# Layer block on one core: a new prologue, a new order in the two short steps, and reciprocals spread by one float32r product

## The reference

```
a   = layernorm(x)
q, k, v = a Wq + bq, (a Wk + bk) Wc We, (a Wv + bv) Wc We      # 16 query heads, 4 key/value heads of 16
qf, kf  = elu(q) + 1, elu(k) + 1
num = einsum(qf, cumsum_t(kf * v));  den = einsum(qf, cumsum_t(kf)) + 1e-6
y   = a + (num / den) Wo + bo
x2  = x + layernorm(y) * gamma + beta
z   = layernorm(x2);  zs = z shifted by one token
xr  = mu_r z + (1 - mu_r) zs;  xk likewise with mu_k
out = x2 + sigmoid(xr W_r^T) * (relu(xk W_k^T)^2 W_v^T)
```

## Time and profile before

| | |
|---|---|
| median of 3 runs | 298.79 us (298.68 to 300.03) |
| the profiled execution's own time | 300.61 us |
| its span in the trace | 298.8 us |
| PE, PEld busy | 272.9 us (91%), 192.7 us (65%) |
| DVE busy | 235.1 us (79%) |
| ACT, POOL busy | 145.4 us (49%), 128.8 us (43%) |
| mean granted TensorE clock | 0.969 |
| chain that ended last | PE 76%, DVE 10%, ACT 5%, issue 3%, DMA 2% |

### The profile page before, as it was taken

One profiled execution on the slowest core, in us unless ns is written; L12 is line 12 of the kernel. 1 busy time (PEld: TensorE's weight loads), 2 busy tenths in 40 slices (PEclk: granted clock), 3 DMA queues, 4 the chain that ended last, 5 costly groups with the idle time before them and its releaser, 6 DMA issues.

```text
span 298.8 us, 7425 instructions
## 1 busy us (share of the span) xinstructions
PE 272.9 (91%) x2923; PEld 192.7 (65%) x2923; DVE 235.1 (79%) x578; ACT 145.4 (49%) x294; POOL 128.8 (43%) x151
## 2 busy tenths in 40 slices
PE   7598798887899999999999999999999999977894
PEld 7565655745685578756885588557865677654663
DVE  6629569799799959996899779985999558989433
ACT  1238655545454756376455844484247520453540
POOL 2711660244474447436753567354344414063310
PEclk9789799997799999999999999999999999999999
DMA  6900202002000013000400020001100110002012
GB/s 175 274 12 3 72 1 72 2 3 70 3 2 0 2 37 105 2 3 3 140 2 0 2 73 0 2 2 35 37 5 0 37 37 2 0 0 71 35 37 70
DMA packets 12178, 10.73 MB, mean 36 GB/s; under 512 B 2288, under 2 KB 12144, under 8 KB 12144
## 3 DMA queue, kind: packets, MB, share of 16 engines
q1 hardware_dynamic: 11392, 9.97, 10.5%
q10 hardware_dynamic: 752, 0.30, 0.4%
HBM read 6.07 MB, written 4.19 MB: 34 GB/s over the span
## 4 chain that ended last, share of the span: by engine, by line
PE 76%; DVE 10%; ACT 5%; issue 3%; DMA 2%; ACTq 1%; POOL 1%; DVEq 0%
PE ps_x L448 9%; PE ps_x L478 8%; PE ps_x L370 7%; PE ps_x L463 6%; PE ps_z L419 6%; PE ps_x L470 6%; PE ps_y L440 5%; PE ps_x L364 5%; PE ps_y L435 5%; PE ps_z L470 4%; PE ps_x L456 2%; PE ps_z L463 2%; PE ps_x L357 2%; DVE probs L953 2%; PE ps_z L402 2%
## 5 line engine op out<-in xcount | busy, mean ns | idle before, releaser
L953 DVE TENSOR_TENSOR probs<-ps_z,causal 128x512 f32<-128x512 f32 x64 | 40.8, 679 | 6.7 <-PE ps_z L419 6.7
L273 POOL TENSOR_TENSOR out_tok<-tanh_r,x_tok 128x512 f32<-128x512 f32 x14 | 18.7, 1338 | 27.7 <-DVE tanh_r L1026 27.7
L1026 DVE SCALAR_TENSOR_TENSOR tanh_r<-tanh_r,ps_x 128x512 f32<-128x512 f32 x13 | 8.9, 687 | 27.0 <-PE ps_x L478 27.0
L448 PE MATMUL ps_x<-wo_sb,oT 128*128 128x256 f32 x128 | 29.6, 382 | 0.0
L250 POOL TENSOR_TENSOR xb_tok<-x_in,beta_bc 128x1024 f32<-128x1024 f32 x8 | 18.9, 2361 | 24.8 <-DVE x_tok L999 24.8
L370 PE MATMUL ps_x<-aT,wq_sb 128*128 128x512 f32 x60 | 27.8, 604 | 0.0
L478 PE MATMUL ps_x<-wvT,k_act 128*128 128x256 f32 x104 | 25.6, 389 | 1.0 <-ACT k_act L773 1.0
L243 POOL TENSOR_TENSOR abo_tok<-a_tok,bo_bc 128x1024 f32<-128x1024 f32 x8 | 18.9, 2360 | 17.3 <-issue 12.6
L217 POOL TENSOR_TENSOR neg_mean<-mv,neg_one 128x4 f32<-128x4 f32 x16 | 5.0, 311 | 49.4 <-DVE mv L884 49.4
L448 PEld LDWEIGHTS ps_x<-wo_sb,oT 128*128 128x128 f32 x128 | 23.6, 190 | 3.8 <-issue 0.9
L213 POOL TENSOR_TENSOR rstd<-rstd,neg_half 128x4 f32<-128x4 f32 x24 | 24.9, 1037 | 1.9
(11 more groups left out here) (133 smaller groups left out, 584.2 us busy)
## 6 DMA issues: line engine op xcount, KB each, us to landing
x_in<-in_L_attn_x_dram SPq DMA_DIRECT2D x8, 512.0 KB, 4.3
out_dram<-out_tok SPq DMA_DIRECT2D x16, 256.0 KB, 2.1
xr<-in_L_attn_Wq_dram ACTq DMA_DIRECT2D x1, 256.0 KB, 4.0
xk<-in_L_ffn_W_r_dram SPq DMA_DIRECT2D x1, 256.0 KB, 5.4
xk<-in_L_ffn_W_k_dram SPq DMA_DIRECT2D x1, 256.0 KB, 5.7
xr<-in_L_ffn_W_v_dram SPq DMA_DIRECT2D x1, 256.0 KB, 7.2
wo_sb<-in_L_attn_Wo_dram SPq DMA_DIRECT2D x4, 64.0 KB, 4.8
bo_bc<-in_L_attn_bo_dram SPq DMA_DIRECT2D x1, 128.0 KB, 5.5
```

Source lines behind the costliest of these rows:

```text
L448: last = mm(bk_[:, (b % 2) * D:(b % 2 + 1) * D], oT[m % 2][:, a, b, :], wo_sb[:, a, :], start=(a == 0), stop=(a == 1))
L953: V.tensor_tensor(probs[b % 2][:, 2 * h:2 * h + 2, :].rearrange("p g (r s) -> p g r s", s=HALF), ps_z[:, 2 * h:2 * h + 2, 0:2 * P].rearran ...
```

## The change

Three parts.

1. **Prologue.** ACT no longer waits for the query loads first: the copies for the key/value weights and `aT` go ahead of it. DVE forms the bias operand before it normalises chunk 0, and the query biases after the statistics of chunk 1. POOL waits for DVE's `a_tok` of chunk 0 before it builds `causal` and `head_rows`, and then builds twice as many pieces of `head_rows` and a new column `low_rows`. DVE waits for these (`pool_const` 2), copies `head_rows` to float32r, and then takes the keys and values of chunk 0.
2. **Short steps.** In steps 0 and 1 DVE follows an order of its own (`short_step`), POOL adds `bo` and `beta` after the denominators' products and the second norm, PE takes `scores(0, 1)` ahead of the transposes of a feed-forward weight. In all steps ACT copies the spread reciprocals between its two copies of `aT`.
3. **Reciprocals.** The second 16 of the 32 columns of `head_cols` now repeat the heads, so the 32 rows of a batch hold each denominator twice. DVE rounds the reciprocals to float32r (`rden_high`) and forms `rden_parts = low_rows * rden_high + rden`: in the first 16 rows the reciprocal, in the second 16 what the rounding lost. One float32r product with `head_rows_r` (ones for both rows) sums them, in place of the float32 product.

The diff, cut to its core:

```diff
+        low_rows = sb("low_rows", 1)
+        rden_high, rden_parts, head_rows_r = (... F32R tensors of (P,), (P,), (2, P))
 POOL, step
-                if c == 0:
-                    pool.wait_ge(s_kf, 2 * n + 2)
-                add_bo(n)
-                add_beta(n)
                 if f >= 0:
+                    add_bo(n)
+                    add_beta(n)
                     second_norm(m)
                     denominator_terms(n)
-                elif m >= 0:
-                    denominator_terms(n)
-                    second_norm(m)
+                else:
+                    if m >= 0:
+                        denominator_terms(n)
+                        second_norm(m)
+                    else:
+                        pool.wait_ge(s_kf, 2 * n + 2)
+                    add_bo(n)
+                    add_beta(n)
 POOL, prologue
             norm_x(0)
+            pool.wait_ge(s_a, 4)
             link(PL.memset(causal[:], 1.0))
 ...
             for b in range(NB):
                 rows = head_rows[32 * b:32 * b + 32, :, :].rearrange("p a (n d) -> p a n d", d=HD)
-                last = PL.affine_select(out=rows, ..., base=0, ...)
+                for r in range(2):
+                    link(PL.affine_select(out=rows, ..., base=-16 * r, ...))
+            link(PL.memset(low_rows[:], -1.0))
+            for b in range(NB):
+                part = low_rows[32 * b:32 * b + 32, :]
+                last = PL.affine_select(out=part, in_=part, compare_op=ALU.is_ge, fill=0.0, base=-16,
+                                        pattern=[[0, 1]], channel_multiplier=1)
                 if b < NB - 1:
                     link(last)
             last.then_inc(pool_const, 1)
 PE
-                        last = mm(banks[b][:, a * P:(a + 1) * P], head_rows[rows, a, :], rden[rows, :],
+                        last = mm(banks[b][:, a * P:(a + 1) * P], head_rows_r[rows, a, :], rden_parts[rows, :],
 ...
-                else:
+                scores(c, 1)
+                if m < 0:
                     pe.wait_ge(ffn_w_in, FFN_IN)
                     pe.wait_ge(s_qf, 2)
                     ffn_weight(0, x1)
-                scores(c, 1)
 ...
-            keep_busy(2)
+            keep_busy(1)
 ACT, step
-                a_out(n)
+                a_out(n, 0)
                 reciprocals(c)
+                a_out(n, 1)
 ACT, prologue
+            act.wait_ge(prep_ps, 1)
+            copy(wcT ...), copy(wkvT ...); act.wait_ge(prep_ps, 2); copy(cewe ...)
+            act.wait_ge(prep_ps, 3); copy(wkv_sb ...), copy(bkv_bc ...)
+            a_out(0, 0)
+            a_out(0, 1)
             act.wait_ge(q_in, Q_IN)
             (the two copies to wq_sb)
-            (the copies above, with a_out(0) ahead of prep_ps 3)
-            act.wait_ge(dve_const, 1)
+            act.wait_ge(dve_const, 2)
 DVE, reciprocal
-                V.reciprocal(rden[:], rden[:]).then_inc(s_rden, 1)
+                V.reciprocal(rden[:], rden[:]).then_inc(s_rf, 1)
+                dve.wait_ge(s_rf, 2 * n + 1)
+                V.tensor_copy(rden_high[:], rden[:]).then_inc(s_rf, 1)
+                dve.wait_ge(s_rf, 2 * n + 2)
+                V.scalar_tensor_tensor(out=rden_parts[:], in0=rden_high[:].bitcast(F32), scalar=low_rows[:, 0:1], in1=rden[:],
+                                       op0=ALU.mult, op1=ALU.add).then_inc(s_rden, 1)
 DVE, steps 0 and 1
+            def short_step(c, n, m):
+                if m >= 0:
+                    add_residual(m, 0, x1)
+                    add_residual(m, 1, x2)
+                mask(c, 1)
+                keys_values(n)
+                key_features(n)
+                divide(c, 0)
+                mask(c, 2)
+                queries(n, 0, x0)
+                if m >= 0:
+                    centre(m)
+                queries(n, 1, x1)
+                divide(c, 1)
+                states(n)
+                key_sums(n)
+                if m < 0:
+                    denominator_terms(n)
+                mask(c, 3)
+                if m >= 0:
+                    second_residual(m)
+                divide(c, 2)
+                if m >= 0:
+                    second_stats(m)
+                reciprocal(n)
+                divide(c, 3)
 DVE, prologue
-            dve.wait_ge(q_in, Q_IN)
-            (neg_bq, bq_1)
+            dve.wait_ge(bias_in, BIAS_IN)
+            dve.wait_ge(dve_const, 1)
+            (bkv_lhs)
             norm_x_scale(0)
-            (the wait for bias_in and dve_const 2, bkv_lhs)
             norm_x(1)
+            dve.wait_ge(q_in, Q_IN)
+            (neg_bq, bq_1)
+            dve.wait_ge(pool_const, 2)
+            V.tensor_copy(head_rows_r[:], head_rows[:])
             dve.wait_ge(prep_sb, 3)
             keys_values(0)
```

More of the change, by code:

```diff
@@ L11 @@
 F32 = mybir.dt.float32
+F32R = mybir.dt.float32r
 AX_X = mybir.AxisListType.X
@@ L93, in build @@
         rden, rden_bc = sb("rden", P), pair("rden_bc", NB, 2, P)
+        low_rows = sb("low_rows", 1)
+        rden_high, rden_parts, head_rows_r = (ctx.enter_context(nc.sbuf_tensor(name, [P, *shape], F32R)) for name, shape in (
+            ("rden_high", (P,)), ("rden_parts", (P,)), ("head_rows_r", (2, P))))
         tail = pair("tail", NB, 2, HD)
@@ L684, in copy, with a_out @@
                 return AC.activation(dst, src, ACT.Copy, **kw)
-            def a_out(n):
+            def a_out(n, k):
                 if n >= 1:
                     act.wait_ge(s_q_ps, 2 * n)
-                for k, bk_ in ((0, x2), (1, x0)):
-                    act.wait_ge(s_aT_ps, 2 * n + k + 1)
-                    copy(aT[:, k, :], bk_[:, :]).then_inc(s_aT, 1)
+                act.wait_ge(s_aT_ps, 2 * n + k + 1)
+                copy(aT[:, k, :], (x2, x0)[k][:, :]).then_inc(s_aT, 1)
             def keys(n):
@@ L841, in _ @@
                     act.dma_start(dst, src).then_inc(q_in, 16)
+            act.wait_ge(prep_ps, 1)
+            copy(wcT[0:64, :], z0[0:64, 0:64])
+            copy(wkvT[0:64, :, :].rearrange("p i n -> p (i n)"), z1[0:64, :]).then_inc(prep_sb, 1)
+            act.wait_ge(prep_ps, 2)
+            copy(cewe[0:64, :], z0[0:64, 128:128 + KV]).then_inc(prep_sb, 1)
+            act.wait_ge(prep_ps, 3)
+            copy(flat(wkv_sb), ps_y[:, 0:256])
+            copy(bkv_bc[:], ps_y[:, 256:384]).then_inc(prep_sb, 1)
+            a_out(0, 0)
+            a_out(0, 1)
             act.wait_ge(q_in, Q_IN)
@@ L1035, in step @@
                     norm_x(n + 1)
-                if f >= 0:
-                    token_shift(f, 0, *for_r)
-                    token_shift(f, 1, *for_r)
+                if f < 0:
+                    short_step(c, n, m)
+                    return
+                token_shift(f, 0, *for_r)
+                token_shift(f, 1, *for_r)
+                add_residual(m, 0, x1)
[8 more added lines that the diff above has]
+                queries(n, 0, x0)
+                token_shift(f, 0, *for_k)
+                token_shift(f, 1, *for_k)
+                queries(n, 1, x1)
[5 more added lines that the diff above has]
+                divide(c, 2)
+                gate(f, 0, x1)
+                reciprocal(n)
+                divide(c, 3)
+                gate(f, 1, x2)
+            def short_step(c, n, m):
                 if m >= 0:
@@ L1043, in step @@
                 keys_values(n)
-                if m >= 0:
-                    centre(m)
                 key_features(n)
-                if m >= 0:
-                    second_residual(m)
                 divide(c, 0)
@@ L1051, in step @@
                 queries(n, 0, x0)
-                if f >= 0:
-                    token_shift(f, 0, *for_k)
-                    token_shift(f, 1, *for_k)
+                if m >= 0:
+                    centre(m)
                 queries(n, 1, x1)
@@ L1057, in step @@
                 states(n)
-                if f >= 0:
-                    second_stats(m)
-                    key_sums(n)
-                else:
-                    key_sums(n)
-                    if m < 0:
-                        denominator_terms(n)
-                    else:
-                        second_stats(m)
-                mask(c, 3)
-                divide(c, 2)
-                if f >= 0:
-                    gate(f, 0, x1)
+                key_sums(n)
+                if m < 0:
+                    denominator_terms(n)
+                mask(c, 3)
+                if m >= 0:
+                    second_residual(m)
+                divide(c, 2)
+                if m >= 0:
+                    second_stats(m)
                 reciprocal(n)
                 divide(c, 3)
-                if f >= 0:
-                    gate(f, 1, x2)
             def finale(c):
@@ L1127, in _ @@
                 V.tensor_reduce(row_mask[:, j:j + 1], head_cols[:, 0, j:8:2], AX_X, ALU.add)
-            dve.wait_ge(q_in, Q_IN)
-            V.tensor_scalar(neg_bq[:], bq_col[:], -1.0, None, ALU.mult)
-            V.tensor_scalar(bq_1[:], bq_col[:], 1.0, None, ALU.add).then_inc(dve_const, 1)
```

(17 more changed lines are left out.)

24 lines of the change are left out of this document (8 added, 16 removed).

## The result

The changed kernel takes **303.87 us** (303.35 to 304.16, 4 runs) where the kernel before takes 298.74 (298.08 to 300.03, 4 runs): a ratio of 1.0164 [1.0128, 1.0201]. I had forecast 300.9 with a range up to 303.0. The direction was right, the size was not: it lies 3.0 above the forecast and 0.9 above the range.

A forecast was written before the change was run, and what follows sets the result against it. PE and DVE together were taken to bound the long steps; earlier, a chain between engines. Prologue -1.7, step 0 +1.9, steps 1 and 2 +2.2, long steps -0.3 make +2.1: 302.7 profiled, 300.9 us median, range 296.8 to 303.0.

The forecast's parts named there:

- the prologue's gain: Prologue: keys of chunk 0 2.5 us earlier, less 0.8 for PE's clock, a gain of 1.7 (0.1 to 2.8).
- the step from the profiled execution to the median: Whole kernel: profiled execution lies 1.8 us above the median of runs, so 302.7 becomes 300.9.
- steps 1 and 2: Steps 1 and 2: POOL's late sums delay `dz`, DVE can't catch up, PE waits at `mix_k`: +2.2 us (-0.4 to 3).
- That PE and POOL's constants bound the prologue: Prologue: DVE waits for POOL's constants, ending at 17.3; keys at 17.7 to 18.7 instead of 20.48.
- the late end: Prologue: float32r copy of `head_rows` takes up to 1.2 us if POOL's zeroing of `zT` holds it; keys at 18.7.
- +0.8 for the clock: Prologue: PE's fallen clock lengthens the second `queries` products by 0.8 us (0 to 1.7).
- the fourth rival: The prologue gives nothing (half clock through second `queries`, copy behind `zT`), or both stalls longer: 302.5 to 303; chance 0.12.
- After waits of 2 to 3 us the clock had fallen in each of the old dips: Prologue: premise from the kernel before's dips, used to expect a lower PE clock after its gap; 0.8 us taken.
- Step 0, the stall: Step 0: `rden_parts` waits behind POOL's `xb_tok`, 2.75 us later than `rden`; the step loses 1.9 (0.7 to 2.1).
- My 1.5 for the new orders of PE and ACT: Step 0: early copy of reciprocals and `scores(0, 1)` ahead of a weight's transposes alone gain about 1.5 us.
- The long steps: Steps 3 to 6: the product falls from 0.72 to 0.36, but DVE's `queries` limit the gain to 0.3 us.
- the slack: Long steps: PE can start `mix_k` only some 0.08 us earlier before DVE's second `queries` holds it.

The follow-up runs named there:

- The filler: Changed kernel plus 36 PE products of zeros in its prologue gap behind the first queries: 302.68 us, ratio 1.0094 to the kernel before.
- before_look: The kernel before, unaltered, run again with a second trace: 300.82 us, ratio 1.0015.
- after_bo_early: Changed kernel with POOL's `abo_tok` sum of step 1 made before the second norm: 304.02 us, ratio 1.0149 to the kernel before.
- after_old_step1: Changed kernel with DVE's and POOL's old order in steps 0 and 1: 301.2 us, ratio 1.0059 to the kernel before.
- all_mended: Changed kernel, DVE's and POOL's old step order, POOL's constants spread over pauses, `head_rows` copy moved, `xb_tok` of chunk 0 held: 295.14 us, 0.9842 to the kernel before.

## Why the prediction was wrong

Two terms make most of the miss: the prologue's gain, forecast at -1.7 and measured at +0.06, and the step from the profiled execution to the median, forecast at -1.8 and measured at -0.3. A third, steps 1 and 2, had the wrong mechanism and came out near by luck.

*That PE and POOL's constants bound the prologue: right in mechanism, the gain mis-sized.* The keys were forecast at 17.7 to 18.7 and came at 18.48, with the copy behind the zeroing as I had it for the late end. The term that failed is the sum after it: I had -2.5 for the keys and +0.8 for the clock, -1.7 together. They are -2.0 and +2.1 (1.66 in the queries and 0.46 in the group before, which I had not counted): 0.06 later. The filler shows the second to be the clock. This is the fourth rival, the clock at half through the second `queries` and the copy behind `zT`, which I had given 0.12; even its 302.5 to 303 lies below what was measured. One premise was wrong as well: "After waits of 2 to 3 us the clock had fallen in each of the old dips" does not hold for step 0, where the waits before it were 0.60 and 1.15, and in *before_look* the clock stayed full behind the same two waits.

*Step 0, the stall: right.* `rden_parts` 2.31 long, ending with `xb_tok`, PE idle 3.76, all as written. The step cost 2.4 for 1.9: the keys product ended at 39.95, and I had 38.3 to 39.6. Those bounds don't come out of my own terms: at full clock they add up to at least 38.6, and with the keys product at half, 3.62 where the runs show it, to over 40. My 1.5 for the new orders of PE and ACT was read from an execution in which step 0 had a low clock; against the one at full clock the short orders give 0.56.

*Steps 1 and 2: the size near by luck, the mechanism wrong.* I had +2.2 from POOL's sums ahead of `dz`; it was +1.45. The centring in 1.67, the residual stalled behind POOL's `prod` and `dz` behind `xb_tok` are all in the trace. What failed is "From there to the second `queries` DVE has no pause in which to catch up, and PE waits with `mix_k`". PE itself was late by then, because its clock was at half from 76 to 86, so `dz` was only 0.7 later against the spread product than before. I had named that low clock and put it "under this one"; it is where the time goes: +1.72 from `z_tok` to `wo_sb`, -0.40 before it and +0.13 behind it make the 1.45. *after_bo_early* shows that `dz` costs nothing; *after_old_step1* shows that the new orders cost about 1% in all. That the clock itself falls for longer because the products on `z_tok` come after one more wait, 1.07, is what the trace suggests; no run took that wait away alone.

*The long steps: right that DVE holds PE, the slack mis-sized.* In a long step of the changed kernel:

```profile
134.85 0.74 DVE L930 SCALAR_TENSOR_TENSOR qf<-ps_x,bq,eq 128x512 f32<-128x512 f32 x1
...
135.64 0.30 PEld L478 LDWEIGHTS ps_x<-xk,wkT 128*128 128x128 f32 x2 [0.20 <-DVE qf L930]
```

The product went from 0.72 to 0.43, a gain of 0.29; PE's weight load now follows DVE's end by 0.05, where I had allowed 0.15 from another pair. So 0.21 a step was to be had and not 0.08: -0.83 for -0.3.

*From the profile to the median: wrong.* I took 1.8 off, as the profiled execution of the kernel before lay that far above its median. That of the changed kernel lies 0.3 above its own. The median of 298.79 came from three runs; in the later sets, of 17 to 23 runs, the kernel before has 299.95 to 300.5, and 300.61 is ordinary. Part of its excess was low clock in step 0 (0.93), which the changed kernel has in both of its profiled executions. An offset between one execution and a small median is not a property that carries over.

The 3.0 of the miss: +1.76 prologue, +0.49 step 0, -0.75 steps 1 and 2, -0.53 long steps, +0.33 the finale, where PE's clock dips once more, +0.15 around the span, and 1.5 for the median, which makes 2.95.

The Trainium skill ("SBUF — State Buffer", on the shared port pair) has a VectorE instruction with two SBUF inputs and a GpSimd instruction that reads SBUF exclude each other: the one that starts second is blocked for the whole instruction of the other. The trace agrees with it in size and place: 2.31 for 0.35 in step 0, 2.80 for 1.67 in step 1. Whether the copy of `head_rows` is a case of the same lock is open: it took 1.13 beside POOL's zeroing and 0.26 with POOL idle in *all_mended*, but its record starts 0.03 ahead of the zeroing, and the rounding, whose record starts as far ahead of `xb_tok`, took its 0.23.

## What to carry to other kernels

A cheaper product is worth what its operands cost to make: here half the records gave 0.21 us in each long step, and the constants, the copy and two short instructions in front of it took away a prologue's whole gain and stalled behind another engine. Where a change makes PE wait longer ahead of a group on the path, put the whole price of the half clock in the sum, for each group up to the return of the full clock (2.1 us in the prologue here, 1.7 in step 2). Idle products in the gap can buy it back, but follow the gain to a later landmark: here 0.36 of 1.85 us was left at `mix_k` of step 2 until the next stall was mended too, and then 3.5. When the runs of a kernel spread by 1 or 2%, look at which dips of the clock the profiled execution has, and where it lies among the runs, before taking a stretch from it as typical or subtracting its distance from the median.

## What the runs showed of the hardware

- A float32r product of 32x128 by 128 columns has one record where the float32 one has two: 8 in 0.43 at full clock for 16 in 0.72. The range that I gave went from a quarter of the time to all of it, and it is 0.6.
- The 36 products of filler took 4.18 of PE and the granted clock reads 1.00 from 12 to 30 us, where without them it reads 0.50 from 18 us on in the trace shown above: a gain of 1.85 us at `prod`, of which 0.36 is left at `mix_k` of step 2.
- A rounding copy of 128x256 on DVE took 1.13 beside a POOL zeroing of 0.96, in all eight traces where they lie side by side, and 0.26 with POOL idle; one of 128x128 took 0.23 though POOL's sum started 0.03 behind it. The records don't tell who held the port in the first case.
